# A mixture-of-experts layer on one core: when the row scatters wait, and where three small pieces of TensorE work stand in line

## The reference

```python
x = x + 0.5 * _L0_ffn_ref(_layernorm(x))    # adapter feed-forward ("f1")
x = x + _L0_attn_ref(_layernorm(x))         # attention
x = x + 0.5 * _L0_ffn_ref(_layernorm(x))    # adapter feed-forward ("f2")
x = x + 0.5 * _L1_ffn_ref(_layernorm(x))    # mixture of experts ("m1")
x = x + _L1_attn_ref(_layernorm(x))         # selective scan ("ss")
x = x + 0.5 * _L1_ffn_ref(_layernorm(x))    # mixture of experts ("m2")
```

```python
scores = sigmoid(xf @ gate_w + bias)
top_scores, top_idx = top_k(scores, 2)                    # 2 of 8 experts for each of 4096 tokens
top_scores = top_scores / (sum(top_scores) + 1e-06)
w = zeros((T, 8)).at[arange(T)[:, None], top_idx].add(top_scores)
up = einsum('th,ehi->tei', xf, up_w) + up_b               # 128 -> 512
eo = einsum('tei,eih->teh', gelu(up), down_w) + down_b    # 512 -> 128
combined = einsum('teh,te->th', eo * 0.1, w)
shared = (gelu(xf @ sw_up + sb_up) @ sw_down + sb_down) * 0.1
out = shared + combined
out = out / (max(abs(out), axis=-1) + 1e-06)
```

## Time and profile before

| | |
|---|---|
| three runs | 1468.17 us median (1465.01 to 1469.24) |
| the profiled execution | 1468.73 us, its span 1466.9 us |
| TensorE, VectorE, ScalarE, GpSimd busy | 89%, 66%, 56%, 37% of the span |
| TensorE's granted clock over the span | 0.942 |
| m1, from its first product to the barrier behind it | 643.1 to 915.6 us |
| m2, to the end | 1208.5 to 1466.9 us |

### The profile page before, as it was taken

The page is one execution under the profiler, slowest core; times in us unless marked ns, Lnnn a source line. Parts: engine busy times, 40 slices in busy tenths (PEclk is TensorE's granted clock), DMA queues, the critical chain, the costliest instruction groups (busy, mean ns, idle before and its releaser), DMA issues. The chain is left out here.

```text
span 1466.9 us, 27761 instructions
## 1 busy us (share of the span) xinstructions
PE 1310.2 (89%) x8392; PEld 711.5 (49%) x8392; DVE 961.6 (66%) x2045; ACT 814.4 (56%) x1727; POOL 547.1 (37%) x746
## 2 busy tenths in 40 slices
PE   2896899999999969879999996899999879999997
PEld 1672222222222237757779874122222136779975
DVE  4787689898889718752223367599999955123337
ACT  0230688888888833444346654566765445435642
POOL 4121332213331021245305402788888744403510
PEclk9995899999999979979999998699999979999999
DMA  5820121222212010021137420444444402116722
GB/s 112 130 88 1 66 77 35 76 76 80 67 49 77 13 20 16 2 58 47 46 94 217 123 70 19 147 159 150 152 138 147 149 22 82 50 43 202 198 63 73
DMA packets 133377, 125.86 MB, mean 86 GB/s; under 512 B 30763, under 2 KB 98297, under 8 KB 133256
## 3 DMA queue, kind: packets, MB, share of 16 engines
q1 hardware_dynamic: 126592, 115.63, 27.8%
q0 software_dynamic: 4544, 8.47, 1.7%
q10 hardware_dynamic: 2120, 0.28, 0.2%
HBM read 90.35 MB, written 31.34 MB: 83 GB/s over the span
## 5 line engine op out<-in xcount | busy, mean ns | idle before, releaser
L1195 DVE TENSOR_REDUCE at_nm<-at_mx 128x2 f32<-128x1024 f32 x256 | 303.9, 1220 | 40.7 <-PE at_mx L1038 39.4
L1141 ACT ACTIVATE at_probs<-at_ring 128x512 f32<-128x512 f32 x512 | 269.4, 605 | 47.5 <-PE at_ring L1050 45.8
L1560 ACT ACTIVATE m_hidden<-m_pU,m_up_b 128x512 f32<-128x512 f32 x192 | 131.2, 687 | 118.6 <-PE m_pU L1805 118.4
L1812 PEld LDWEIGHTS m_pD<-m_down,m_hidden 128*128 128x128 f32 x1536 | 177.4, 192 | 17.7 <-issue 17.7
L2354 POOL TENSOR_TENSOR ss_hc<-ss_h,ss_c_all 128x512 f32<-128x512 f32 x128 | 161.8, 1271 | 51.1 <-DVE ss_h L2524 43.8
L1805 PE MATMUL m_pU<-m_xT_all,m_up 128*128 128x512 f32 x384 | 175.6, 604 | 2.5 <-DVE m_yt L1786 1.4
L1812 PE MATMUL m_pD<-m_down,m_hidden 128*128 128x128 f32 x1536 | 177.6, 275 | 0.0
L1050 PE MATMUL at_ring<-at_qq,at_kk 51*128 51x512 bf16 x512 | 163.4, 387 | 7.0 <-ACT at_probs L1141 6.0
L1038 PE MATMUL at_mx<-at_kk,at_qq 48*128 48x512 bf16 x512 | 156.0, 398 | 13.5 <-DVE at_nm L1195 8.9
L2524 DVE TENSOR_TENSOR_SCAN ss_h<-ss_pA,ss_beta 128x512 f32<-128x512 f32 x128 | 155.2, 1215 | 13.8 <-issue 6.1
L1531 POOL DMA_INDIRECT pair_rows<-m_y,m_y_id x78 | 75.7, 970 | 174.0 <-DVE m_y L1790 174.0
(11 more groups left out here) (347 smaller groups left out, 1990.6 us busy)
## 6 DMA issues: line engine op xcount, KB each, us to landing
ss_dtb<-ss_dt_rows SPq DMA_DIRECT2D x128, 256.0 KB
m_up_now<-in_L_ffn_up_w_dram SPq DMA_DIRECT2D x54, 256.0 KB, 3.2
at_qq<-q_stack SPq DMA_DIRECT2D x64, 96.0 KB, 2.2
at_kk<-k_stack SPq DMA_DIRECT2D x64, 96.0 KB, 2.3
m_hidden<-in_L_ffn_up_w_dram SPq DMA_DIRECT2D x24, 256.0 KB
sorted_rows<-empty_row SPq DMA_DIRECT2D x2, 2535.0 KB, 23.7
m_down_all<-in_L_ffn_down_w_dram SPq DMA_DIRECT2D x16, 256.0 KB, 4.5
m_up_now<-pair_rows SPq DMA_DIRECT2D x16, 256.0 KB, 3.0
```

The source lines that it names most:

```text
L1141: act.activation(probs[:, (slot % 2) * GH + ORDER[j], :], ring[bank][:, :], ACT.Exp, scale=SCALE).then_inc(s.exp_done, 1)
L1195: dve.tensor_reduce(nm[group % 2][:, 2 * (pair % 2) + parity, 2 * half:2 * half + 2], mx[parity][:, :, :], AX.X, ALU.max, negate=True).the ...
L1560: act.activation(hidden[t % 2][:, k, :], pU[k][:, :], ACT.Gelu, bias=up_b[buf][:, k:k + 1]).then_inc(s.gelu_done, 1)
L1812: last = pe.matmul(pD[t % 2][:, c, :], hidden[t % 2][:, k, c * P:(c + 1) * P], down[buf][:, k, :], start=(k == 0), stop=(k == NI - 1))
```

## The change

Three edits, all inside `moe_ffn`, of both layers except the third, which acts only where the scan's inputs are made (m1).

- The scatters of one choice count up one semaphore (`scattered[k]`), and none of them waits for another. GpSimd waits for all 16 of the first choice before `mark(1)`, as before, and SyncE for all 16 of each.
- RANK_AT goes from 1 to 2 and COUNT_AT from 4 to 5.
- In `expert`, the down products of a sequence are issued ahead of `scan_lead_pe`.

```diff
-RANK_AT, COUNT_AT = 1, 4
+RANK_AT, COUNT_AT = 2, 5
...
             for i in range(SCATTERS):
-                sp.wait_ge(scattered[i], 16 * (2 * HT // SCATTERS))
+                sp.wait_ge(scattered[i], 16 * HT)
...
             def scatter(k, t):
-                n = k * HT + t
-                if n >= SCATTERS:
-                    pool.wait_ge(scattered[n % SCATTERS], 16 * (n // SCATTERS))
                 pool.indirect_dma_start(sorted_rows, bass.IndirectOffsetOnAxis(ap=index[:, k, t:t + 1], axis=0),
                                         v.rows[:, t, :], None, bounds_check=HB * P - 1, oob_is_err=False
-                                        ).then_inc(scattered[n % SCATTERS], 16)
+                                        ).then_inc(scattered[k], 16)
...
             for t in range(HT):
                 scatter(0, t)
-            wait_scattered(HT)
+            pool.wait_ge(scattered[0], 16 * HT)
             mark(1)
...
                     if t == 1:
                         pe.wait_ge(s.shared_acc, NB)
-                    if lead is not None and (last == 1 or last == 0 and t < ND):
-                        scan_lead_pe(pe, g, q=ahead, s=lead, t=ND * last + t)
                     if t > 0:
                         pe.wait_ge(pD_free[(t - 1) % 2], ND // 2 * n - ND // 2 + (t - 1) // 2 + 1)
                         down_product(n, buf, t - 1)
+                    if lead is not None and (last == 1 or last == 0 and t < ND):
+                        scan_lead_pe(pe, g, q=ahead, s=lead, t=ND * last + t)
```

More of the change, by code:

```diff
@@ L1514, in mark @@
                 pool.wait_ge(s.marked, k + 1)
-            def wait_scattered(n):
-                for i in range(SCATTERS):
-                    pool.wait_ge(scattered[i], 16 * (n // SCATTERS))
             def scatter(k, t):
-                n = k * HT + t
-                if n >= SCATTERS:
-                    pool.wait_ge(scattered[n % SCATTERS], 16 * (n // SCATTERS))
                 pool.indirect_dma_start(sorted_rows, bass.IndirectOffsetOnAxis(ap=index[:, k, t:t + 1], axis=0),
                                         v.rows[:, t, :], None, bounds_check=HB * P - 1, oob_is_err=False
-                                        ).then_inc(scattered[n % SCATTERS], 16)
+                                        ).then_inc(scattered[k], 16)
             def put(j):
```

## The result

The changed kernel took 1518.64 us (median of 4 runs, 1514.61 to 1523.11) against 1468.49 us (4 runs, 1465.01 to 1469.24): a ratio of 1.034, 95% interval 1.032 to 1.037. The forecast was 1464.3. (All ratios here are estimates from every single run of both kernels, and need not equal the quotient of the two medians.) The profiled execution of it took 1514.61 us.

What follows compares the result with a forecast made beforehand. TensorE, busy 89% of the span, was taken as the bound, with m1's end set by the last engine at the barrier. Terms -3.0 - 0.9 + 0 + 0 + 0 = -3.9 us gave 1464.3 us, range 1460.5 to 1468.

Steps and rivals of the forecast that it cites:

- the scatters' term of 0: MoE layers: 30 scatter waits, 33.8 us in all, disappear, about 17 us a layer from GpSimd's idle time; gain 0.
- the one cover: Scatters: last issued at 715.74, SyncE's first read of sorted rows at 752.30, a slack of 36 us.
- The ranks in m1: m1's start: without TensorE's wait for VectorE's `both`, a gap of 3.48 less 0.47 for the ranks' passes, gain 3.0 us.
- In m2: m2's start: the same removal of the ranks' wait, 1.39 - 0.47, gain 0.9 us.
- Both distances between starts: Ranks' gains built from weight-load-to-product distances, 3.9 us for both layers, chosen over the traced idle time of 2.55 us.
- The lower bound, 2.55 us for both layers: Ranks: only the idle time traced to the wait comes back, 2.32 us in m1 and 0.23 in m2.
- The count: m1's start: count moved one sequence later, list ready at about 680, cost 0 with 11 us of cover.
- The slower rival: Denser scatters delay the first listed expert's weights beyond 4.4 us of cover; 1472.3 us if the landing trebled; chance 0.07.
- The down products at m1's end: m1's end: VectorE ends 1.9 to 3.8 us earlier, but SyncE's transfers come last at 913.6; term 0.0.
- The bound of +1.2: m1's end: cost if `lift` is later by the full 3.66 us and ScalarE's slack is lost.
- The chance of 0.55 for no difference: Whole kernel: 0.30 of the forecast, 0.23 for a smaller ranks' gain, 0.03 of the weights rival, rounded.
- 0.05 for slower: Whole kernel: 0.04 from scatters delaying the weights, 0.01 for an unnamed disturbance.

Runs made afterwards that it cites:

- the clean run: The changed kernel itself, unedited, run again on chip 4, where nothing stalled: 1465.42 us (8 runs), ratio 0.9998 to the kernel before.
- the flood: The changed kernel with one more scatter of the same 128 rows, to unread memory, ahead of each scatter, on chip 14: 1471.98 us, ratio 1.003.
- chip 14's: The changed kernel once more, unedited, on chip 14: 1467.18 us (10 runs), ratio 0.9996 to the kernel before.
- that with 64 rows: Scatters without waits, writing 64 of each tile's 128 rows, against the kernel before: 1466.57 us on chip 7, 1529.90 us on chip 10.

## Why the prediction was wrong

**The step that failed is the scatters' term of 0.** It took the 17 us a layer from GpSimd's idle time, named the one cover (36 us until the first read), and priced the denser transfers by what they could delay, the first listed expert's weights. That they could hold up engines that neither wait for them nor share a transfer with them was in no term. It measured 140.3 - 115.7 = 24.6 us in m1 against the clean run and 142.0 - 116.5 = 25.5 us in m2; 1.5 of the 24.6 lie at m1's start, ahead of the ranks, and are the clock's (see the ranks below), so the stall in m1 is 23 us.

What the runs show of it: 
- It goes with the chip, or with the visit to it. Kernels with scatters 1.2 to 1.3 us apart took at most 1480.2 us in all 79 executions on chips 4, 7, 9, 12 and 14, and at least 1499.9 us in all 10 on chips 2 and 10 and in the first measurement. So it is not chance from one execution to the next. The kernel before, whose scatters are 1.8 us apart in the mean ((715.74 - 659.16) / 31 in m1), shows it nowhere (3 executions on chip 2, 1 on chip 10, 4 in the first measurement).
- It builds up. TensorE's first gap of over 0.4 us without a releaser begins with the 11th to 13th scatter (676.4 in the first measurement, 676.5 and 670.0 and 670.8 on chip 2, 671.8 on chip 10), some 14 to 16 us after the first. GpSimd's pause of 3 us between a layer's two halves buys a few microseconds: on chip 2, with the scatters' edit alone, 20 down passes run without a gap from 679.12 to 683.28, and from 683.9 on the gaps are back.
- It doesn't go by rows, as far as the one run on chip 10 says, nor by the DMA engines, whose share is 0.10 to 0.17 in it, and the scatters land on time in it. Nor do the blocks of instructions that DMA brings come late: in the two layers' stretches with scatters these transfers took 0.3 to 1.5 us each in the changed kernel, 0.4 to 1.4 us on chips 2 and 10, and 0.5 to 1.4 us in the clean run.

The reading that fits is a backlog of something small that each scatter adds to, drained at a rate that differs between chips, and that lies between one scatter per 1.27 us (1.21 on chip 10) and one per 1.8 us on chips 2 and 10. That is argued, not shown, and the cause stays open: that a wider spacing without waits is free of it there wasn't tried on a chip that stalls, and what backs up is not seen in any row. The clock of 0.5 to 0.68 in it is no first cause, since it falls behind the first gaps (0.90 and 1.00 in the stretches in which they begin), but it adds to the loss: TensorE's products take longer until it rises.

The Trainium skill has one candidate. "NOTIFIC — the notification-queue block", section "7.1 Overflow: three behaviours, one of which stalls the engine", says that the block which writes the engines' records holds its producers back rather than lose a record inside, and names a counter of stalls that would tell whether it had throttled an engine. By it the loss would be one of recorded executions only. No run here can show it, since every execution that was timed also has records.

**The other terms, from runs without the stall.** The ranks in m1: forecast -3.0, measured 118.3 - 115.7 = -2.6 in the clean run. Two executions with that edit gave this (115.7 and 115.8 us to the first block), but four others only -1.0 to -1.6 (116.7 to 117.4). What differs is when TensorE's clock rises. It is at 0.50 when m1 begins, and reaches 1.00 2.9 to 3.0 us behind m1's first product in the first two, 4.9 us behind it in the two with 116.7 and 6.1 to 6.2 us in the two with 117.4. The first six microseconds of m1 in the clean run and in the kernel with the ranks and the count alone, the granted clock third from the right:

```profile
642.65:645.65 3.00, 3.00 (x4) 1.42 (x5) 2.83 (x6) 2.96 (x4) 2.69 (x5) 0.52 0.44 123
645.65:648.65 3.00, 3.00 (x8) 1.33 (x7) 2.83 (x6) 2.64 (x5) 2.51 (x7) 1.00 0.95 268
```

```profile
640.91:643.91 3.00, 3.00 (x4) 1.45 (x5) 2.83 (x6) 2.96 (x4) 2.69 (x5) 0.50 0.56 163
643.91:646.91 3.00, 3.00 (x4) 1.04 (x4) 2.83 (x6) 1.86 (x3) 2.51 (x7) 0.50 0.79 232
```

Eight products run in the second three microseconds of the clean run, and four in the other. In kernels with the ranks at their old place it makes no difference (118.33 us with the rise at 2.9 us, 118.34 at 6.1), since TensorE waits for `both` anyway. So the wait that the change removes hid a late rise of the clock. The prediction took its distances from an execution in which the rise came at 2.9 us, and had no term for it coming later. In the first measurement the rise came at 5.9 us. In m2: forecast -0.9, measured 116.9 - 116.5 = -0.4. Both distances between starts promised more than came. The lower bound, 2.55 us for both layers, was passed in two of the six executions (2.9 and 2.8) and missed in four (1.3 to 2.4).

The count: 0, and no wait of TensorE's at it. The first listed expert's last load was issued at 692.81 in the clean run and landed in 4.1 us, as in the earlier trace rows; in the stalled run the same load took 3.4 us. The slower rival's mechanism didn't occur, though its sign did.

The down products at m1's end: forecast 0.0, measured +1.2 to +1.3 in every kernel with that edit but the flood (155.4 or 155.5 us; without it 153.8 to 154.2). The rows of the changed kernel, to be read against the earlier trace rows:

```profile
916.38 1.12 PE L2096 MATMUL ss_zy<-ss_dt_low,ss_w_dtp 64*128 64x512 f32 x2
...
917.54 0.69 ACT L2143 ACTIVATE ss_edt<-ss_zy,ss_b_dtp 128x512 f32<-128x512 f32 x1 [2.64 <-PE ss_zy L2096]
...
919.64 1.29 DVE L1719 TENSOR_SCALAR m_most<-m_most 128x4 f32<-128x4 f32 x1
920.97 4.39 DVE L1723 SCALAR_TENSOR_TENSOR X<-m_acc,m_most,X 128x128 f32<-128x128 f32 x4
...
925.62 7.58 SPq L2027 DMA_DIRECT2D ss_stack<-ss_parts  x12
...
927.07 2.05 DVE L1756 SCALAR_TENSOR_TENSOR m_acc<-m_out_b,m_w_listed,m_acc 128x128 f32<-128x128 f32 x4 [0.15 <-DVE m_out_b L1750]
...
931.74 0.86 DVE L96 BATCH_NORM_STATS2 bn<-X 128x6 f32<-128x128 f32 x4
...
936.48 1.28 ACT L2442 ACT_TABLE_LOAD   x1 [9.01 <-PEq L2601]
```

Up to SyncE's last transfer the working held: in the clean run `lift` starts at 893.66, which with the 3.1 us that its blocks were early (761.5 against 758.4) is 896.76, against 896.75 forecast; the last issue ends at 910.48 + 3.1 = 913.6, as forecast. VectorE ends before it (932.60 against 933.20 here), if later than forecast, since a step of its chain for the last sequence but one takes 4.39 us beside GpSimd's products and 1.14 us without. But the scan began 3.28 us after SyncE's last issue (936.48 - 933.20), where I had taken over the 1.97 us that lay behind VectorE's last instruction. That difference, 1.31, is the whole of the miss. It lies at the end of SyncE's own list. Without this edit the other engines pass the barrier at the end of `moe_ffn` 0.28 us behind VectorE's last instruction. With it they pass 1.66 us behind SyncE's last issue, which is 0.71 us behind the end of the last packet of that transfer (934.15), and the same two numbers come back in five of the six other executions with the edit. So SyncE seems to reach the barrier only when its last transfer has landed; that is read from the constant distance, and no run separates it. In the flood the engines passed 2.6 us later than that, for a reason that isn't known. (The bound of +1.2 for this term works out as 914.7 - 913.64 = 1.1 from its own numbers.)

The sum of the terms where nothing stalls is -2.6 - 0.4 + 1.2 = -1.8 us with the early rise of the clock (chip 4's trace) and -1.6 - 0.3 + 1.2 = -0.7 us on chip 14's, against medians of -2.2 (chip 4) and -0.4 (chip 14) and ratios that include 1. The chance of 0.55 for no difference described that world; 0.05 for slower left the other out.

No version was clearly faster than both kernels. Where the stall comes the kernel before is the fastest measured, by 2 to 3%; where it doesn't, the ranks and the count alone, with neither the scatters' edit nor the move at m1's end, came out the same as it (0.9998), since what they save (1.3 us in that trace) is less than the spread of the scan.

## What to carry to other kernels

A wait that nobody's critical path contains can still be what keeps a kernel out of trouble: here its removal cost 3% in the first measurement and on chip 2. By the reading above it held one queue to a pace, and so limited what that queue adds to something shared and unseen. Removing a wait on which the profile puts a cost of 0 buys nothing, so there is nothing to set against such a risk; take away waits that somebody waits behind, and leave the rest. And a result of one chip is one sample: measure an edit that makes a queue denser on several, and when several engines of a program stall at once for nothing that the profile shows, try the same program elsewhere before taking it apart.

## What the runs showed of the hardware

- The same program took 1465 to 1467 us on two chips and 1518 us on another, where the kernel before differed by less than 1 us between them.
- GpSimd's indirect transfer of 128 rows of 520 bytes holds it 0.97 us and one of 64 rows 0.91, so rows cost next to nothing; between two on end lie 0.30 us; the landing takes 2.4 us in the median.
- Of 16 scatters issued on end, all had landed 2.35 us after the last issue even while TensorE, ScalarE and VectorE were stalled.
- The stage behind the barriers starts 1.97 us after VectorE's last instruction in the kernel before, and 3.28 us after SyncE's last issue in the changed one (3.3 in six executions with that edit, 5.6 in the flood).
- TensorE's clock was at 0.50 at m1's start, and rose to 1.00 between 2.9 and 6.2 us behind the first product, from execution to execution. With the ranks' wait gone this moves m1's length by 1.6 us.
- The scan has two lengths, 291 to 294 us and 297 to 299 us, by the execution and not by the edit: the kernel with waits four places in front has 292.8 in one trace and 298.5 in another, that with 64 rows 292.3 and 298.9 (the kernel before has runs up to 1477 too). Two stretches of it, first in the kernel with the scatters' edit alone on chip 9 (293.6 us), then in that with the two others (299.0 us); the third column from the right is TensorE's clock:

```profile
960.00:1000.00 40.00, 37.27 (x115) 9.74 (x114) 38.70 (x51) 26.59 (x46) 34.84 (x30) 1.00 0.53 162
1040.00:1080.00 40.00, 35.87 (x105) 9.16 (x104) 38.08 (x54) 27.73 (x52) 32.98 (x27) 0.99 0.46 152
```

```profile
960.00:1000.00 40.00, 37.41 (x105) 8.95 (x104) 35.66 (x46) 24.48 (x43) 31.72 (x26) 0.91 0.48 147
1040.00:1080.00 40.00, 38.88 (x95) 9.27 (x96) 30.71 (x40) 24.20 (x47) 28.63 (x25) 0.79 0.37 122
```

VectorE does 30.71 us of work instead of 38.08 in the second stretch, with TensorE's mean clock at 0.79. The difference between the two lengths, 5 us or more in most pairs, is larger than every gain that this change could bring.
